# The first residual of a decoder step moved behind its last score maximum, the second ahead of x1's normalising

## The reference

```
x1 = layernorm(x + mixer(x) + x)                 # a gated convolution with a small scan, projected by W_out; it adds x itself too
x2 = layernorm(x1 + attention(x1, ctx))          # 16 heads of width 16, keys and values from ctx
x3 = layernorm(x2 + experts(x2))                 # router, 8 experts of capacity 640; an overflowing token keeps x2
layernorm(v) = (v - mean(v)) / sqrt(var(v) + 1e-5)
```

## Time and profile before

| | us |
|---|---|
| median of 3 runs | 891.89 |
| lowest and highest | 891.1 and 897.04 |
| the profiled execution | 892.89 |
| its span, first to last instruction | 891.1 |

### The profile page before, as it was taken

How to read it: one execution, slowest core, us unless ns; L and a number is a source line. 1 busy time by engine, 2 the same in 40 slices (tenths; PEclk the granted TensorE clock), 3 DMA queues, 4 the chain that set the end, 5 groups by cost and what they waited for, 6 DMA issues and landing times. The chain is left out here.

```text
span 891.1 us, 16520 instructions
## 1 busy us (share of the span) xinstructions
PE 799.7 (90%) x5722; PEld 628.8 (71%) x5722; DVE 594.9 (67%) x1452; ACT 403.1 (45%) x644; POOL 351.6 (39%) x288
## 2 busy tenths in 40 slices
PE   8998987788998999999999998875799999999993
PEld 6776765556666666666766665544699999999993
DVE  5889873556877777777787777644266666666653
ACT  5665642145554555555655546551244234423420
POOL 1332353333344444545445533224321454245423
PEclk9999997889999999999999999886699999999997
DMA  4112912544354644545545534130512433243100
GB/s 132 48 47 60 296 54 70 157 144 139 118 163 124 173 120 128 157 125 158 159 118 134 153 101 143 60 112 27 177 48 90 126 118 105 90 134 123 50 19 31
DMA packets 76081, 100.93 MB, mean 113 GB/s; under 512 B 11065, under 2 KB 63522, under 8 KB 76024
## 3 DMA queue, kind: packets, MB, share of 16 engines
q1 hardware_dynamic: 72568, 92.06, 34.7%
q0 software_dynamic: 3456, 8.13, 2.5%
HBM read 65.47 MB, written 35.74 MB: 114 GB/s over the span
## 5 line engine op out<-in xcount | busy, mean ns | idle before, releaser
L1301 DVE TENSOR_REDUCE nmax<-ps_m 128x4 f32<-128x1024 f32 x128 | 156.6, 1224 | 50.5 <-PE ps_m L881 38.4
L1099 ACT ACTIVATE pt<-ps_a 128x1024 f32<-128x1024 f32 x128 | 131.4, 1027 | 99.6 <-PE ps_a L891 75.8
L1574 ACT ACTIVATE hid<-ps_h 128x640 fp32r<-128x640 f32 x64 | 45.1, 705 | 147.0 <-PE ps_h L1502 147.0
L1502 PE MATMUL ps_h<-xt,w_hi 128*128 128x320 f32 x512 | 101.4, 321 | 1.0 <-DVE xt L1589 1.0
L881 PE MATMUL ps_m<-kst,qst 48*128 48x256 f32 x512 | 66.1, 337 | 28.1 <-DVE nmax L1301 24.3
L1624 DVE SCALAR_TENSOR_TENSOR hid<-ps_h,hid 128x640 fp32r<-128x640 f32 x64 | 52.8, 825 | 49.2 <-ACT hid L1574 48.7
L1674 POOL DMA_INDIRECT out_rows<-gated,token x40 | 49.9, 1247 | 88.6 <-issue 88.6
L881 PEld LDWEIGHTS ps_m<-kst,qst 48*128 48x128 f32 x512 | 39.6, 190 | 63.5 <-DVE nmax L1301 33.8
L1502 PEld LDWEIGHTS ps_h<-xt,w_hi 128*128 128x128 f32 x512 | 80.6, 193 | 4.2 <-DVE hid L1624 2.4
L757 POOL TENSOR_TENSOR half<-kq,half 128x512 fp32r<-128x512 f32 x32 | 41.5, 1296 | 100.9 <-ACT half L1065 100.9
L1516 PE MATMUL ps_y<-w,hid 128*128 128x512 f32 x320 | 80.1, 392 | 0.0
(11 more groups left out here) (206 smaller groups left out, 1602.7 us busy)
## 6 DMA issues: line engine op xcount, KB each, us to landing
halves_dram<-half SPq DMA_DIRECT2D x64, 256.0 KB, 2.5
gated<-in_w SPq DMA_DIRECT2D x16, 1024.0 KB, 5.1
kst<-halves_dram SPq DMA_DIRECT2D x64, 128.0 KB, 2.7
qst<-halves_dram SPq DMA_DIRECT2D x64, 128.0 KB, 3.0
rows_dram<-blank SPq DMA_DIRECT2D x1, 5160.0 KB, 22.3
gated<-rows_dram SPq DMA_DIRECT2D x7, 645.0 KB, 4.3
x_raw<-in_x_t SPq DMA_DIRECT2D x8, 512.0 KB, 3.9
xres<-in_x SPq DMA_DIRECT2D x16, 256.0 KB, 3.4
```

The costliest lines, as they stand in the source:

```text
L1099: nc.scalar.activation(pt[:, k % 4].rearrange("p s t q -> p (s t q)"), ps_a[:].rearrange("p s t q -> p (s t q)"), ACT.Exp).then_inc(s["exp ...
L1301: nc.vector.tensor_reduce(nmax[:, q, :, :, h // 2].rearrange("p t s -> p s t"), ps_m[:], AX.X, ALU.max, negate=True).then_inc(s["max_done" ...
L1502: mm = pe.matmul(ps_h[:, f % 2, c2, 0:HC], w1[a][:, p, k, f * P:(f + 1) * P], xt[:, b, p, k, c2 * HC:(c2 + 1) * HC], start=(n == 0 and k = ...
L1574: nc.scalar.activation(hid[:, HI, f, :].rearrange("p (c n) -> p c n", c=2), ps_h[:, f % 2, :, 0:HC], ACT.Relu).then_inc(s["hid_hi"], 1)
```

## The change

In the VectorE program the mixer residual with its statistics goes from slot 13 to slot 14, behind the maximum that stands there; the attention residual and `var2` go ahead of `x1`, which goes from slot 14 to the end of slot 15. In the GpSimd program root 2 goes ahead of keeping x1. The calculation and the number of instructions stay as they are.

```diff
@@ GpSimd's step @@
                     nc.gpsimd.tensor_tensor(ve1[:], ve1[:], power[:], ALU.pow).then_inc(s["rstd1"], 1)
+            if on(n, 3) and not late:
+                rstd2(n - 3)
+            if on(n, -1):
                 pool.wait_ge(s["x1_done"], n + 2)
                 nc.gpsimd.tensor_tensor(gated[:, 0:KT, bass.ds((n + 1) * S, S)], x1[:],
                                         c["b_o"][:, None, :].to_broadcast([P, KT, D]), ALU.add
                                         ).then_inc(s["x1_kept"], 1)
-            if on(n, 3) and not late:
-                rstd2(n - 3)
@@ VectorE's step @@
-                if h == 13 and on(n, -1) and not first:
+                if h == 14 and on(n, -1) and not first:
                     dve.wait_ge(s["wout_mm"], n + 2)
                     dve.wait_ge(s["x_added"], n + 2)
...
-                if h == 13 and on(n, -1) and not first:
+                if h == 14 and on(n, -1) and not first:
                     mean_var(dc, st1, mv1, s["stats1"], n + 1)
                     nc.vector.tensor_scalar(ve1[:], mv1[:, :, 1], EPS, None, ALU.add).then_inc(s["var1_ready"], 1)
-                if h == 14 and on(n, -1) and not first:
+                if h == 15 and on(n, 3):
+                    residual2(n - 3)
+                if h == 15 and on(n, 3):
+                    var2(oc, n - 3)
+                if h == 15 and on(n, -1) and not first:
                     dve.wait_ge(s["rstd1"], n + 2)
...
                     op.then_inc(s["x1_done"], 1)
-                if h == 15 and on(n, 3):
-                    residual2(n - 3)
-                if h == 15 and on(n, 3):
-                    var2(oc, n - 3)
```

## The result

The change makes the kernel slower: 906.69 us median (900.06 to 910.91, 4 runs) against 892.56 for the kernel before on the same chip (891.1 to 897.04, 4 runs), 1.0129 times, with a 95% interval of 1.0086 to 1.0172. Later, on another chip, it was 1.0094 times before (1.0062 to 1.0127). The forecast was 889.5 us, 0.3% faster, and its range ended at 895.5. The profiled execution took 906.13 us, with a span of 904.3.

The account below looks back on a forecast made before the run. VectorE's work from r1 to maximum 0 was taken to bound each turn; -3.8 (full turns) - 0.5 (loop jump) + 1.8 (lead-in) = -2.5 us from the 891.89 median, stated as 889.5 us, range 884.5 to 895.5.

Parts of the forecast that it names:

- The full turns: Steps 4 to 14: maximum 7 no longer waits behind r1, maximum 0 comes 0.32 us earlier; 3.8 us gained in all.
- The jump of the loop: After steps 7, 9 and 11: x1 may hide the idle time before maximum 0; 0.5 us gained, bounds 0 and 1.0.
- The lead-in: Steps 0 to 3: r1 never waited for x2b there, so the new order only loses; 1.8 us lost.
- The rival of a slow lead-in: Steps 1 and 2: more TensorE idle time leaves stretches at the lower clock, adding 3.6 us, to 893.0; chance 0.12.
- the second point under the full turns: Full turns, GpSimd: root 2 comes in time for `pay`, and keeping x1 later behind it delays nobody; no loss.
- x1 collides with root 2: Steps 3 to 14: x1 waits for root 2 running beside it, 0.71 us each, 8.5 us, to 897.9; chance 0.05.

Follow-up runs that it names:

- e2: The changed kernel, but GpSimd keeps x1 only behind the split of the next keys; 891.65 us, 0.9946 times the kernel before.
- e6: The changed kernel with VectorE's old order in steps 0 to 2; 1.0077 times the kernel before.
- changed_again: The changed kernel, unaltered, measured once more on another chip; 1.0094 times the kernel before.
- e7: The changed kernel with keeping x1 behind the key split and VectorE's old order in steps 0 to 2; 889.19 us, 0.9927 times the kernel before.
- e1: The changed kernel, but GpSimd's split of the keys also waits until `ve3` is done; 895.25 us, 0.9996 times the kernel before.
- e8: The kernel before with GpSimd's part of the change alone, root 2 ahead of keeping x1; 1.0142 times the kernel before.
- e5: The changed kernel with `ve3` made by two instructions of one element instead of one of two; 896.43 us, 1.0011 times the kernel before.
- e3: The kernel before with two more `bn_aggr`, into a tile nobody reads, ahead of `ve3`; 907.18 us, 1.0103 times the kernel before.
- e9: The kernel before with two more `bn_aggr` ahead of `ve3` and the key split waiting for `ve3`; 894.69 us, 0.9995 times the kernel before.
- e11: The changed kernel, keeping x1 behind the key split, old VectorE order in steps 0 to 2, split waiting for `ve3`; 890.63 us, 0.9947 times before.

## Why the prediction was wrong

The views of before were read rightly as far as they were read. Point by point:

- *The full turns.* Forecast: maximum 0 is 0.32 us earlier. Measured: 0.30 at step 14, the keys at 2.52 us behind scores 7 against 2.49 before, scores 1 with a wait of 0.59 (forecast 0.65). With the collisions gone (e2) the turn from step 8 to step 12, where the granted clock is 1.00 in both profiles, is 26.36 us against 26.84 before: 0.48 less, as the forecast's 0.32 and 0.18 of the jump (half of 0.37, which comes at every second turn) would have it. e2's whole time is 0.5% below before (0.3 to 0.8), where the forecast had 0.3%.
- *The jump of the loop.* Forecast: 0 to 0.35 us each. Maximum 0 after step 7 has no idle time in front of it now, so the whole 0.37 of the earlier trace rows is hidden behind x1, as the row below shows: it has no idle time at its end. The Trainium skill, Advanced Engine Details and Errata, section Control Flow Timing, gives 108 ns for a compare-and-branch, which is less than the 0.37 us that is hidden here.

```profile
349.74 1.22 DVE L1302 TENSOR_REDUCE nmax<-ps_m 128x4 f32<-128x1024 f32 x1
```

- *The lead-in.* Forecast 1.8 us lost, 1.35 of it in steps 1 and 2. The mechanism was right: x1 waits 0.82 us for root 1 in both steps, and at the end of step 1 it takes 188.34 - 183.70 = 4.64 us from maximum 7 to maximum 0, forecast 183.58 - 178.93 = 4.65:

```profile
183.70 1.23 DVE L1302 TENSOR_REDUCE nmax<-ps_m 128x4 f32<-128x1024 f32 x1 [1.13 <-PE ps_m L882]
...
187.69 0.73 DVE L1350 TENSOR_SCALAR x<-r,mv,ve 128x256 f32<-128x256 f32 x2 [0.82 <-POOL ve L800]
188.34 1.22 DVE L1302 TENSOR_REDUCE nmax<-ps_m 128x4 f32<-128x1024 f32 x1
```

The size isn't settled. Giving steps 0 to 2 their old order back gains 1.4 us (e6 against changed_again) or, by the ratios, 1.7 us (e7 against e2), neither clear of the noise. The output projection of step 3 starts at 233.6 us on average in the six profiles with the new lead-in and at 230.2 in the eight with the old, 3.4 us apart, but the profiles of a group spread over 5 us. The changed kernel's own profile was 1.8 us late already at r1 of step 0, in front of which nothing was changed.
- *The rival of a slow lead-in* had 0.12. From 144 to 235 us the granted clock is 0.82 on average in those six profiles and 0.86 in the eight, so it may have a part in the 3.4 us; which part was not separated.
- *The step that failed* is the second point under the full turns: "Behind it on GpSimd's queue stands keeping x1, now later than before", and "nobody needs `gated` for three steps", from which follows "From scores 1 on both engines run as before". What comes behind scores 1 was thus put at nothing. I asked who waits for the moved instruction, and not what runs beside it. Beside it runs pay, and pay takes 0.89 us instead of 0.73. With these 0.16 us `ve3` misses a lead of 0.04 to 0.12 us over the key split and takes 1.18 us instead of 0.17 in most of 12 steps. No row ahead of the prediction showed that lead, because I did not line VectorE up with GpSimd behind maximum 0. Of that 1.0 us VectorE can hide a part: with `ve3` freed (e1) the turn from step 8 to step 12 is 26.68 us, against 27.24 in changed_again, so about 0.6 us a turn is what the held `ve3` costs, with the later split of e1 counted in.
- *The rival.* "x1 collides with root 2" had the right mechanism and the wrong pair. x1 started first there, and GpSimd's root was the one to stretch, 0.80 us instead of 0.71. It was given 0.05 on an argument that fell: that x1's pace, 256 elements in 0.33 us, shows that it does not use both ports. pay has the same form and pace, and is held (e8). The rule of the Trainium skill, SBUF — State Buffer, section Who interferes with whom, was the better guide without my condition: `tensor_scalar` is in its list of what can take the shared pair, two SBUF inputs contend with GpSimd's reads, and issue order decides who is blocked. The traces agree on all three: with pay and `ve3` (0.89 us instead of 0.73, 1.18 instead of 0.17), with y (2.68 instead of 1.67, e5), and with `ve3` in e1 and e3, where it is short when it starts first and long when the split does.

The account of a turn, an estimate from turns at full clock: from maximum 0 to maximum 2 +1.19 us (0.16 in pay, 1.0 in `ve3`). VectorE's 0.52 us wait for the router's logits covers part, the block comes 0.30 sooner, and the jump gives back 0.18 on average: +0.2. From step 8 to step 12 the turn was 26.84 us before and is 27.24 in changed_again, +0.4. More than the rest is in `hot` (0.51 us a pair in the changed kernel's profile and 0.64 in changed_again, against 0.36) and in the cast (0.24 against 0.17). They run beside GpSimd's `twice`, but did so in the kernel before too; why they are longer was not tested. Eleven turns give 4 to 5 us and the lead-in 1.4 to 3.4, together 6 to 8, against the 8.4 (= 0.0094 x 895.6) that changed_again lost.

Part of the loss goes with the clock, and the lead-in's may overlap with it. In the 52 runs of the kernel before that lie beside the experiments, 0.01 less mean granted clock goes with about 3.2 us more time. changed_again's four runs have 0.940, against 0.946 for the ten of the kernel before on its chip: by that some 2 us of its loss go with the lower clock and 6.4 don't, again an estimate. The first measurement's 14 us hold more of it: its four runs of the changed kernel have 0.936, and the profile of the kernel before 0.948. Whether the new order itself lowers the clock was not separated.

## What to carry to other kernels

When an instruction of VectorE or GpSimd is moved, lay the two engines' timelines side by side from there to the next place where both wait, and look for pairs that touch SBUF together; who starts first decides, and here a lead of 0.05 us saved VectorE 1 us and the turn some 0.6. Moving the GpSimd instruction away takes the collision out. A semaphore wait that fixes the order of the pair does too, cost nothing measurable here (e9, e11), and keeps the order from hanging on small delays. And ask of each instruction that goes later not only who waits for it, but whom it will now stand beside.

## What the runs showed of the hardware

- A `tensor_scalar` of 2 elements a partition, 0.17 us by itself, took 1.18 us when a GpSimd `tensor_tensor` of 512 elements (1.28 us) had started 0.12 us before it, 0.99 at 0.31 us (e8) and 0.83 at 0.46 (changed): each time it ended as the GpSimd instruction did. Cut in two instructions of one element each it was not held at all (0.15 us, e5).
- A `tensor_scalar` with two per-partition scalars, SBUF to SBUF, 256 elements, is held too: a pair took 1.40 us instead of 0.73 where the GpSimd instruction had started 0.36 us before (e8). Yet undisturbed the second of a pair follows 0.33 us behind the first, one element in 1.3 ns, the pace at which the residual's 512 elements pass in 0.68 us.
- GpSimd's instruction suffers less in the opposite order: 0.80 instead of 0.71 us for root 2, and 1.36 to 1.59 instead of 1.27 for the split of the queries beside y (the 1.59 in e11).
- 0.17 us of added work made the whole kernel 1.0% slower (e3), and one more wait took that away (e9).
